# A quantised MLP stage written out as one unrolled program with tiles in groups of four

## The reference

```python
x = x + _L0_ffn_ref(_layernorm(x, axis=-1), w_gate, w_up, w_down)

def _weight_quant(w):
    scale = 1.0 / jnp.clip(jnp.mean(jnp.abs(w)), 1e-05)
    return jnp.clip(jnp.round(w * scale), -1.0, 1.0) / scale
def _act_quant(x):
    scale = 127.0 / jnp.clip(jnp.max(jnp.abs(x), axis=-1, keepdims=True), 1e-05)
    return jnp.clip(jnp.round(x * scale), -128.0, 127.0) / scale
def _bitlinear(x, w):
    return jnp.einsum('bsi,oi->bso', _act_quant(x), _weight_quant(w))

gate = jax.nn.silu(_bitlinear(x, w_gate))
up = _bitlinear(x, w_up)
return _bitlinear(gate * up, w_down)
```

## Time and profile before

| | us |
|---|---|
| median of 3 runs (range) | 2974.94 (2969.46 to 2979.68) |
| profiled execution | 2967.82 |
| its span | 2966.0 |
| stage `l0_ffn` in it, 2033.30 to 2152.71 | 119.4 |
| of it normalisation, 2033.30 to 2046.10 | 12.8 |
| quantising x and weights, 2046.10 to 2066.60 | 20.5 |
| first loop and scales, 2066.60 to 2103.79 | 37.2 |
| second loop and end, 2103.79 to 2152.71 | 48.9 |

### The profile page before, as it was taken

How to read it: one execution, slowest core, us unless ns; L and a number is a source line. 1 busy time by engine, 2 the same in 40 slices (tenths; PEclk the granted TensorE clock), 3 DMA queues, 4 the chain that set the end, 5 groups by cost and what they waited for, 6 DMA issues and landing times. The chain is left out here.

```text
span 2966.0 us, 35240 instructions
## 1 busy us (share of the span) xinstructions
PE 2491.8 (84%) x11867; PEld 1410.3 (48%) x11875; DVE 2271.7 (77%) x3096; ACT 1871.8 (63%) x2593; POOL 890.7 (30%) x494
## 2 busy tenths in 40 slices
PE   6689999998899999999999999995445666556998
PEld 3356666663344444444444444432235564444675
DVE  4487777773899999999999999984679995654443
ACT  4365555554799888899888888884345553123443
POOL 1021111111444444444344444440020002003665
PEclk8889999999899999999999999997566777557999
DMA  1000000001000000000000000000000101110000
GB/s 55 8 25 18 15 16 18 15 4 74 6 0 3 33 0 36 0 36 0 36 0 36 0 36 1 0 0 11 0 27 29 35 29 56 44 40 17 26 8 15
DMA packets 23168, 60.10 MB, mean 20 GB/s; under 512 B 2864, under 2 KB 14960, under 8 KB 21616
## 3 DMA queue, kind: packets, MB, share of 16 engines
q1 hardware_dynamic: 23024, 58.29, 5.7%
HBM read 53.04 MB, written 5.24 MB: 20 GB/s over the span
## 5 line engine op out<-in xcount | busy, mean ns | idle before, releaser
L251 PE MATMUL a_ps<-a_x,a_w 128*128 128x512 f32 x1536 | 695.6, 598 | 24.8 <-DVE a_kf L599 12.5
L251 PEld LDWEIGHTS a_ps<-a_x,a_w 128*128 128x128 f32 x1536 | 291.5, 191 | 404.4 <-issue 367.8
L774 POOL TENSOR_TENSOR a_den<-a_qf,a_ksum 128x1024 f32<-128x1024 f32 x128 | 271.2, 2119 | 510.3 <-DVE a_qf L592 473.7
L777 POOL TENSOR_TENSOR a_num<-a_qf,a_kvsum 128x1024 f32<-128x1024 f32 x128 | 295.0, 2304 | 186.1 <-DVE a_kvsum L617 185.9
L2281 DVE TENSOR_REDUCE x_rn<-x_sqk 128x8 f32<-128x512 f32 x256 | 174.3, 681 | 105.6 <-ACT x_sqk L2205 101.5
L2205 ACT ACTIVATE x_sqk<-x_b_k 128x512 f32<-128x512 f32 x256 | 153.1, 598 | 156.7 <-PE x_b_k L2117 150.2
L262 PE MATMUL a_ps<-a_att,a_w 128*128 128x512 f32 x480 | 215.8, 592 | 0.0
L2098 POOL TENSOR_TENSOR x_kn<-x_craw,x_w 128x256 f32<-128x256 f32 x64 | 47.0, 735 | 509.6 <-DVE x_craw L2270 488.1
L592 DVE SCALAR_TENSOR_TENSOR a_qf<-a_eq,a_qf 128x1024 f32<-128x1024 f32 x128 | 195.4, 1527 | 1.7
L445 ACT ACTIVATE a_den<-a_den,consts 128x1024 f32<-128x1024 f32 x128 | 147.0, 1149 | 55.3 <-POOL a_den L774 55.3
L599 DVE SCALAR_TENSOR_TENSOR a_kf<-a_ek,a_ps 128x1024 f32<-128x1024 f32 x128 | 155.5, 1215 | 27.9 <-ACT a_ps L441 23.4
(11 more groups left out here) (416 smaller groups left out, 5493.6 us busy)
## 6 DMA issues: line engine op xcount, KB each, us to landing
a_w<-layers SPq DMA_DIRECT2D x8, 2577.0 KB, 9.8
x_craw<-ctx SPq DMA_DIRECT2D x32, 256.0 KB, 2.7
y_cx<-ctx_t SPq DMA_DIRECT2D x16, 512.0 KB, 3.5
m_w<-experts SPq DMA_DIRECT2D x8, 608.0 KB, 3.9
x_w<-xattn_w SPq DMA_DIRECT2D x1, 2048.0 KB, 7.4
x_all<-x_t SPq DMA_DIRECT2D x1, 1024.0 KB, 4.9
t_scratch<-t_q_t SPq DMA_DIRECT2D x4, 256.0 KB, 3.7
t_scratch<-t_k_t SPq DMA_DIRECT2D x4, 256.0 KB, 5.5
```

The lines of the kernel that those rows point to most:

```text
L251: last = nc.tensor.matmul(bank(tile, j), col(par, part * HK + u * P, P), x[:, t0:t0 + BANK], start=True, stop=True)
L774: nc.gpsimd.tensor_tensor(by_batch(den[:, b, :]), by_batch(qf[:, b, :]), bcast(ksum[:, b, :], S), ALU.mult).then_inc(d_ready, 1)
L777: nc.gpsimd.tensor_tensor(by_batch(num[:, b, :]), by_batch(qf[:, b, :]), bcast(kvsum[:, b, :], S), ALU.mult).then_inc(n_ready, 1)
```

## The change

The stage's three blocks become one, in which the program of each engine is written out by Python loops, with no hardware loop. Tiles go in four groups of four (`parts` = 4, `per` = 4). The call of `layernorm_all` is replaced by code of the stage's own with the same steps. What moves between engines: squares from POOL to ACT; the rounding and clipping of the weights from DVE to POOL; the subtraction of `ROUND` from the hidden values to ACT (`to_integer`, with a bias of -`ROUND` that POOL sets at the start), so that DVE clips shifted values in one step; the scaling of down results from DVE to ACT (`scale_y`). What moves in time: the sum of the weights goes ahead of DVE's fourth centring; x is quantised per slice of 512 tokens, each turned back and kept by itself; group p of the results is added after DVE's work on the hidden tiles of group p + 1. PE and ACT interleave the gate and up products and Silus of the next group with the turning, keeping, down product and scaling of this one. PSUM is addressed as eight banks; `h` holds eight tiles instead of sixteen. The diff, cut:

```diff
+            @block.gpsimd
+            def _(pool):
+                nc.gpsimd.memset(unround[:, :], -ROUND).then_inc(cleared, 1)
+                pool.wait_ge(w_scaled, 2)
+                for i in range(3):
+                    nc.gpsimd.tensor_scalar(wr[:, i, :], wf[:, i, :], wscale[:, i:i + 1], ROUND, ALU.mult, ALU.add).then_inc(w_rounded, 1)
+                pool.wait_ge(w_rounded, 3)
+                nc.gpsimd.tensor_scalar(wr[:, :, :], wr[:, :, :], -ROUND, 1.0, ALU.add, ALU.min).then_inc(w_rounded, 1)
+                pool.wait_ge(w_rounded, 4)
+                nc.gpsimd.tensor_scalar(wt[:, :, :], wr[:, :, :], -1.0, None, ALU.max).then_inc(w_set, 1)
...
             @block.tensor
             def _(pe):
+                def gate_up(t):
+                    pe.wait_ge(xq_kept, t // per + 1)
+                    wait_past(pe, h_ready, t - 1)
...
+                def turn_h(t):
+                    pe.wait_ge(h_quant, t + 1)
+                    wait_past(pe, h_kept, t)
...
+                def down(t):
+                    pe.wait_ge(h_kept, t + 1)
+                    wait_past(pe, y_set, t - 1)
...
+                for p in range(parts):
+                    t = per * p
+                    if p == 0:
+                        gate_up(2)
+                        gate_up(3)
+                    if p + 1 < parts:
+                        gate_up(t + 4)
+                        gate_up(t + 5)
+                    if p == 0:
+                        pe.wait_ge(xq_kept, 4)
+                    turn_h(t)
+                    turn_h(t + 1)
+                    down(t)
+                    turn_h(t + 2)
+                    down(t + 1)
+                    turn_h(t + 3)
+                    down(t + 2)
+                    if p + 1 < parts:
+                        gate_up(t + 6)
+                    down(t + 3)
+                    if p + 1 < parts:
+                        gate_up(t + 7)
+                    turn_y(p)
...
             @block.scalar
             def _(act):
+                def to_integer(t):
+                    act.wait_ge(h_clipped, t + 1)
+                    wait_past(act, h_turned, t - 1)
+                    nc.scalar.activation(hq[:, t % 2, :], hr[:, t % per, :], ACT.Identity, bias=unround[:, 0:1]).then_inc(h_quant, 1)
...
+                def scale_y(t):
+                    act.wait_ge(down_done, t + 1)
+                    wait_past(act, y_turned, t // per - 1)
+                    nc.scalar.activation(y[:, t % (2 * per), :], bank(6 + t % 2)[:, 0:P], ACT.Copy, scale=hback[:, t:t + 1]).then_inc(y_set, 1)
...
+                for p in range(parts):
+                    act.wait_ge(centred, p + 1)
+                    nc.scalar.activation(tmp[:, of(p)], xn[:, of(p)], ACT.Square).then_inc(squared, 1)
+                for p in range(parts):
+                    act.wait_ge(var_ready, p + 1)
+                    nc.scalar.activation(tmp[:, of(p)], bank(4 + p), ACT.Ln, bias=eps5).then_inc(logged, 1)
...
+                for p in range(parts):
+                    t = per * p
+                    if p == 0:
+                        silu(2)
+                        silu(3)
+                    if p + 1 < parts:
+                        silu(t + 4)
+                        silu(t + 5)
+                    to_integer(t)
+                    to_integer(t + 1)
+                    keep_h(t)
+                    to_integer(t + 2)
+                    keep_h(t + 1)
+                    scale_y(t)
+                    to_integer(t + 3)
+                    keep_h(t + 2)
+                    scale_y(t + 1)
+                    if p + 1 < parts:
+                        silu(t + 6)
+                    keep_h(t + 3)
+                    scale_y(t + 2)
+                    if p + 1 < parts:
+                        silu(t + 7)
+                    scale_y(t + 3)
...
             @block.vector
             def _(dve):
+                nc.vector.tensor_copy(identb[:, :], ident).then_inc(ident_set, 1)
+                centre(0)
+                centre(1)
+                centre(2)
                 dve.wait_ge(w_loaded, 16)
+                nc.vector.tensor_reduce(wsum[:, :], wf[:, :, :], AX_X, ALU.add, apply_absolute_value=True).then_inc(w_summed, 1)
+                centre(3)
+                normalise(0)
+                weights()
+                for p in range(1, parts):
+                    normalise(p)
+                for p in range(parts):
+                    quantise_x(p)
+                hidden(0)
+                hidden(1)
+                add(0)
+                hidden(2)
+                add(1)
+                hidden(3)
+                add(2)
+                add(3)
```

More of the change, by code:

```diff
@@ L832, in l0_ffn @@
[L832 to L836, removed]
-        with nc.Block() as block:
+        y = sb("y", [P, 2 * per, P])
+        w_loaded, w_summed, w_mean, w_scaled, w_rounded, w_set, cleared, ident_set = (
+            sem(n) for n in ("w_loaded", "w_summed", "w_mean", "w_scaled", "w_rounded", "w_set", "cleared", "ident_set"))
@@ L839, in _ @@
             @block.tensor
             def _(pe):
[L842 to L848, removed]
@@ L849, in _, with mean, var @@
-                for t in range(TILES):
-                    last = nc.tensor.transpose(turned[:, t, :], xq[:, t, :], identb[:, :])
-                last.then_inc(xq_turned, 1)
+                def mean(p):
+                    nc.tensor.matmul(bank(p), ones, x_in[:, of(p)], start=True, stop=True).then_inc(mean_ready, 1)
+                def var(p):
+                    pe.wait_ge(squared, p + 1)
+                    nc.tensor.matmul(bank(4 + p), ones, tmp[:, of(p)], start=True, stop=True).then_inc(var_ready, 1)
@@ new lines, in turn_x, with turn_back @@
+                def turn_x(p):
+                    pe.wait_ge(normed, p + 1)
+                    for t in range(per):
+                        last = nc.tensor.transpose(bank(4 + p)[:, t * P:(t + 1) * P], xn[:, (per * p + t) * P:(per * p + t + 1) * P], ident)
+                    last.then_inc(x_turned, 1)
+                def turn_back(p):
+                    pe.wait_ge(x_quant, p + 1)
+                    for t in range(per):
+                        last = nc.tensor.transpose(half_bank(4 + p)[:, t * P:(t + 1) * P], xq[:, p % 2, t * P:(t + 1) * P], identb[:, :])
+                    last.then_inc(xq_turned, 1)
@@ new lines, in down, with turn_y @@
+                def down(t):
+                    pe.wait_ge(h_kept, t + 1)
+                    wait_past(pe, y_set, t - 1)
+                    for c in range(FCH):
+                        last = nc.tensor.matmul(bank(6 + t % 2)[:, 0:P], hqt[:, t % 2, c * P:(c + 1) * P],
+                                                wt[:, 2, c * P:(c + 1) * P], start=(c == 0), stop=(c == FCH - 1))
+                    last.then_inc(down_done, 1)
+                def turn_y(p):
+                    pe.wait_ge(y_set, per * (p + 1))
+                    wait_past(pe, x_out, p)
+                    for t in range(per):
+                        last = nc.tensor.transpose(bank(5)[:, t * P:(t + 1) * P], y[:, (per * p + t) % (2 * per), :], ident)
+                    last.then_inc(y_turned, 1)
@@ new lines, in _ @@
+                for p in range(parts):
+                    mean(p)
+                for p in range(parts):
+                    var(p)
+                    if p == 2:
+                        pe.wait_ge(w_summed, 1)
+                        pe.wait_ge(centred, 1)
+                        nc.tensor.matmul(bank(0)[:, 0:3], ones, wsum[:, :], start=True, stop=True).then_inc(w_mean, 1)
+                turn_x(0)
+                turn_x(1)
+                turn_x(2)
+                turn_x(3)
+                pe.wait_ge(ident_set, 1)
@@ L870, in _ @@
[L870 to L876, removed]
@@ L885, in _ @@
[L885 to L891, removed]
@@ L892, in _ @@
[L892 to L898, removed]
```

243 lines of the change are left out of this document (122 added, 121 removed).

## The result

The changed kernel takes 2947.05 us (median of 11 runs, 2944.63 to 2959.31), the kernel before 2973.3 (median of 11, 2964.93 to 2983.36). The ratio is 0.9919, 95% interval 0.9901 to 0.9937: by the ratio 24 us less, by the medians 26. The profiled execution took 2945.16 us, its span is 2943.4.

What follows compares the result with a forecast made beforehand. The stage was taken as bound by a chain passing from engine to engine: hidden tiles start at 35.0, first clip 43.1, three periods 46.5, tail 9.9, end 99.5 against 119.4; 20 us off the median gives 2955, range 2940 to 2966.

Steps and rivals of the forecast that it cites:

- the lock: Normalisations and first x slice: DVE instructions wait for POOL's running one; 2.7 to 7.3 us, taken at 5.0.
- the gates for which DVE waits: Steady groups: DVE waits for ACT's gates of tiles 6, 7, 10, 11; about 4 us of each period.
- the entry: Normalisation: squares on ACT precede the logarithms; last normalisation ends at 15.4 instead of 12.8, losing 2.6 us.
- the slices of x: Quantising x on DVE: 3.65 us per slice of 512 columns, four times 14.6 us.
- The periods: Steady groups: PE and ACT hand tiles over in written order; 15.4, then 15.6 us, three periods 46.5.
- the tail: Last group, no Silus between: last scaling 7.9 us after the clip, then turn and addition; 9.9 us.
- first clipped tile: First group of four hidden tiles: 8.1 us after DVE starts on them at 35.0, so at 43.1 us.
- the upper bound from the product of two tensors: Weights' rounding on POOL: 4608 columns at a two-tensor product's 2.2 ns a column, 10 us.
- rival 1: More is gained: small operations slip past POOL, or PE gets 2.4 GHz in the groups; 2942 to 2950, chance 0.18.
- Rival 2: Identity not in Silu's table set: two loads of 1.28 us per group, ten us in sum; 2965, chance 0.08.
- Rival 3: POOL's two-operation tensor_scalar with pointer far slower, DVE held behind it; slower from 7.8 ns a column; 2984 or more, chance 0.03.
- Rival 4: Gain fades elsewhere: another clock in stages behind, or hand-overs 0.3 us more each; 2963 to 2970, chance 0.06.

Runs made afterwards that it cites:

- a3: Changed kernel with the next group's third and fourth gate and up products and Silus earlier in PE's and ACT's queues; stage 86.1 us, median 2941.21, ratio 0.989.
- a7: Changed kernel with PE and ACT doing the next group's four products and Silus only behind this group's results; stage 106.4 us, median 2959.88, ratio 0.9967.
- a2: As a1, with GpSimd executing the same five weight instructions into buffers that nobody reads; stage 98.2 us.
- a9: As a2, with seven other GpSimd instruction forms of 1536 columns for nobody; stage 112.5 us.
- a1: Changed kernel with the weights rounded and clipped on VectorE again, GpSimd only setting the bias; stage 88.7 us.
- a6: Order of a3, weights rounded on ScalarE and clipped on VectorE, no GpSimd; stage 78.2 us, median 2928.44, ratio 0.9839 to the kernel before.
- a8: As a6, with the normalisation's squares on GpSimd again; stage 76.9 us, median 2928.52, ratio 0.9864.

## Why the prediction was right

The forecast was 2955 with a range of 2940 to 2966; 2947.05 lies inside, and the gain is 24 us where 20 were forecast. The mechanisms of the sum came as written: who hands over to whom, the lock, and the gates for which DVE waits. Its sizes were off. The lock was forecast 3.2 us too short, and the entry and the slices of x, forecast 1.7 and 1.2 too long, hid that. The periods were forecast 4.7 us too long and the tail 0.7, and nothing hid these: the stage became 25.5 us shorter and not 19.9. Points are from the stage's start, the others are lengths, in us:

| point | forecast | measured |
|---|---|---|
| last normalisation ends, no lock | 15.4 | 13.7 with it |
| lock | 5.0, with the normalisations | 8.2, in the first slice |
| first hidden multiply | 35.0 | 35.3 |
| first clipped tile | 43.1 | 42.9 |
| three periods | 46.5 | 41.8 |
| tail | 9.9 | 9.2 |
| stage | 99.5 | 93.9 |

**Entry.** The written order was followed and the loss against before was 0.9, not 2.6 us. The step took three means at 1.7 us each; in this execution four took 5.18 us, the third centring started at 4.4 and not 5.5 (2034.61 - 2030.25), because the granted clock rose during the means. In a3 and a7 it rose later: the third centring started at 5.5, as forecast, and the last normalisation ended at 14.8 and 14.9. So 1.1 of the 1.7 us is the clock's moment, and the rest is what the paragraph on the groups finds, lengths added end to end.

**GpSimd.** The mechanism stands, as a2 shows. The size was wrong twice. POOL took 12.7 us, above the 10 us of the upper bound from the product of two tensors, although that row's mean took in one product of 1.42 us among three of 1.04; as a9 shows, a tensor_scalar outside multiply-and-add costs more a column than that product does. And with it the lock took 8.2 us in the first slice, above the slow end of 7.3; the normalisations, which the forecast let slip by 0.4 to 1.9, were stretched by 0.4, 0.2 and 0.1 us and ended 0.1 later than in a1. The middle of two bounds was no safer than either, as the bounds were of other forms. The sentence that nothing could come out below zero was right; what was missing was to set its 5.0 against the 3.3 us that the weights take on DVE; in the trace of before they took 3.5 (2061.66 to 2065.18), so by the forecast's own lock the move already lost. The rule quoted from the Trainium skill (GPSIMD Engine Reference, Engine selection), elementwise work belongs on VectorE, holds here: 88.7 against 93.9. That GpSimd is roughly line-rate on one input, which the prediction took from the same section, does not: 5.70 and 4.09 us where VectorE took 0.96. The same page (Elementwise, side-by-side cycle accounting) gives 1.03 cycles an element, and of the forms measured only multiply and add in a9 comes near it (1.0 ns a column, 1.2 cycles); for the others the measurement decides, 2.7 to 3.7 ns.

**Quantising x.** The four slices were taken at 3.65 and took 3.34 (2055.47 to 2058.81): two neighbouring operations of DVE that don't depend on each other overlap by 0.1, and I added them end to end. This 1.2 us and the 1.7 of the entry cancelled the lock's 3.2, which is why the first hidden multiply was met to 0.3 us. That agreement is luck, not insight.

**Groups.** The order of the hand-overs and where DVE waits came as written (DVE's gates of tiles 6, 7, 10, 11, 14, 15; 9.5 us in six waits). The period was 13.95, not 15.4 and 15.6. The failing term is again the sum end to end: the down products start 0.38 us after the turn's start (2092.12, 2092.50), not 0.61, and gate and up 0.43 after the down products; ACT's neighbouring instructions overlap by 0.1 (2094.03 + 0.69 against 2094.61). Up to the last Silu of a group that is 1.2 us, and DVE's multiply and reduction behind it took 1.5 and not 1.75: 1.4 a group. The 0.2 that the forecast added for the second and third period did not come either, which makes 4.7 in three. The tail is the same sum: its last scaling ended 7.3 us after the clip, not 7.9. The second loop of before had shown the overlap on PE, in two rows of its timeline that I did not use:

```profile
2106.58 0.60 PE L916 MATMUL f_ps<-f_identb,f_hq 128*128 128x128 bf16 x4 [0.71 <-DVE f_hq L976]
...
2106.98 0.63 PE L922 MATMUL f_ps<-f_wt,f_hqt 128*128 128x128 bf16 x4
```

The second starts 0.40 us after the first, whose length is 0.60.

**Rivals.** The clock stayed at 0.50 in the groups and the small operations did not slip past POOL, so rival 1 didn't happen by either of its mechanisms, though the time landed in its band; the clock did rise in a3, a6 and a8. Rival 2 falls: one load of 1.28 us stands ahead of the first Silu (2056.74) and none before an Identity. Rival 3 was right that POOL's tensor_scalar is slower than its other work, with DVE behind it, but at half its price, 2.8 ns a column in the mean and not 5.9, and it named the wrong form: the one with a pointer was the fast one. Rival 4 can't be read from one execution; the medians say no.

## What to carry to other kernels

When work is moved to GpSimd, price what VectorE loses while it runs, not only when the result is needed: here an instruction on four columns waited 4.6 us. When a program is written out by hand for engines that take their queues in order, look for the engine with the most work and see whether its inputs stand behind other engines' late steps; two products and two Silus a group moved forward in their queues were worth 7.8 us of 94. And before a loop is credited with overlap, look in its body for table loads.

## What the runs showed of the hardware that I had not expected

GpSimd's tensor_scalar on 128 x 1536: multiply and add with a pointer 1.55 us, one operation 4.1, two other operations 5.4 to 5.7, the output type making no difference. ACT loaded its table in each of eight passes of the hardware loop of Silus (2067.75 to 2097.00), whose body uses one function only the earlier trace rows, and once when the same loop was written out. It is not so of every hardware loop: the second one of before, whose ACT instruction is a copy, has no load in its eight passes. Not all of DVE is held by a GpSimd instruction: beside the 4.1 us instruction of a9 a reciprocal took 0.18 (2065.98) and a multiply with one operand in PSUM 0.69 us (2066.19), while a tensor_scalar on four columns was held to its end (3.93 from 2062.02). A product of two SBUF operands was held too, for 4.57 us, but ended 0.8 us ahead of the 5.71 us instruction beside it, and the next such product took its plain 0.68 us inside that remainder (2055.43 to 2056.11, the GpSimd instruction from 2050.57 to 2056.28), so there the lock did not last to the recorded end. With the order of a3 the granted clock in the groups rose from 0.50 to between 0.58 and 0.84 in single periods of a3, a6 and a8; in the changed kernel it stayed at 0.50.
